# Four key tiles of a group's product with V at one step of the slot instead of at four

## The reference

```python
q, k, v = layernorm(x) @ Wq.T, context @ Wk.T, context @ Wv.T   # 16 heads of 16 channels
scores = q . k * SCALE, causal mask (keys 0..511 only matter)
probs = softmax(scores); y = probs . v; x = x + tanh(g_xattn) * (y @ Wo.T + bo)
# experts: softmax of layernorm(x) @ gate_w.T, each of 8 experts takes the 128 best tokens of a batch,
# silu(x_in @ w_gate) * (x_in @ w_up) @ w_down, scaled and added back, times tanh(g_ffn)
```

## Time and profile before

| | us |
|---|---|
| median of 3 runs (lowest, highest) | 2138.99 (2138.17, 2143.24) |
| the profiled execution | 2140.27 |
| its span, first to last instruction | 2138.5 |
| PE busy in the span | 1984.6 |
| DVE busy | 1221.2 |
| ACT busy | 956.8 |

### The profile page before, as it was taken

One profiled execution on the slowest core, in us unless ns is written; L12 is line 12 of the kernel. 1 busy time (PEld: TensorE's weight loads), 2 busy tenths in 40 slices (PEclk: granted clock), 3 DMA queues, 4 the chain that ended last, 5 costly groups with the idle time before them and its releaser, 6 DMA issues.

```text
span 2138.5 us, 43770 instructions
## 1 busy us (share of the span) xinstructions
PE 1984.6 (93%) x15339; PEld 1222.1 (57%) x15464; DVE 1221.2 (57%) x2441; ACT 956.8 (45%) x1792; POOL 582.7 (27%) x490
## 2 busy tenths in 40 slices
PE   3899999999999999996599999999999999999997
PEld 2455555555555555553256566565656666665665
DVE  4767787787777777775643434334343434435332
ACT  2456555555556555654243433333333433334332
POOL 2112222222222222213323231323323232322312
PEclk9999999999999999997699999999999999999999
DMA  4543444434444443334222221322222231312212
GB/s 114 116 120 107 131 130 129 116 119 122 131 138 134 127 138 114 112 94 134 63 70 47 53 57 43 64 59 57 48 53 48 72 60 40 60 26 35 40 15 26
DMA packets 141569, 179.70 MB, mean 84 GB/s; under 512 B 23544, under 2 KB 123008, under 8 KB 141440
## 3 DMA queue, kind: packets, MB, share of 16 engines
q1 hardware_dynamic: 116864, 144.39, 22.7%
q0 software_dynamic: 24576, 33.57, 9.7%
HBM read 118.63 MB, written 58.72 MB: 83 GB/s over the span
## 4 chain that ended last, share of the span: by engine, by line
PE 48%; DVE 2%; DMA 1%; issue 1%; POOL 0%; ACT 0%; DVEq 0%; ACTq 0%; POOLq 0%
PE bank L986 10%; PE bank L987 10%; PE bank L985 10%; PE bank L1002 5%; PE bank L1000 5%; PE bank L1001 5%; PE bank L955 2%; PE bank L969 1%; DMA out<-y,row_now 1%; DVE top_at L1061 1%; DVE work L1064 1%; DVE top L1059 1%; DVE h L1108 0%; ACT h L1038 0%; POOL out L919 0%
## 5 line engine op out<-in xcount | busy, mean ns | idle before, releaser
L529 ACT ACTIVATE prob<-bank 128x512 f32<-128x512 f32 x640 | 378.2, 596 | 234.3 <-PE bank L418 223.3
L613 DVE TENSOR_REDUCE mx<-bank 128x1 f32<-128x384 f32 (+3 forms) x704 | 429.7, 635 | 87.9 <-PE bank L402 78.8
L919 POOL DMA_INDIRECT out<-y,row_now x128 | 201.6, 1575 | 705.3 <-ACT y L1046 681.0
L1108 DVE TENSOR_TENSOR h<-bank,silu 128x512 f32<-128x512 f32 x256 | 176.7, 690 | 345.2 <-PE bank L987 283.8
L1038 ACT ACTIVATE h<-h 128x512 bf16<-128x512 f32 x256 | 161.1, 629 | 392.5 <-DVE h L1108 392.5
L400 PE MATMUL bank<-ks,qs 96*128 96x128 bf16 (+3 forms) x1024 | 279.7, 306 | 48.5 <-DVE mx L613 31.0
L1111 DVE TENSOR_TENSOR h<-h 128x512 bf16<-128x512 f32 x256 | 177.3, 693 | 179.3 <-ACT h L1038 179.3
L1000 PE MATMUL bank<-downT,h 128*128 128x256 bf16 x1024 | 279.3, 273 | 0.0
L1002 PE MATMUL bank<-downT,h 128*128 128x256 bf16 x1024 | 279.3, 273 | 0.0
L1001 PE MATMUL bank<-downT,h 128*128 128x256 bf16 x1024 | 279.3, 273 | 0.0
L416 PE MATMUL bank<-qs,ks 98*128 98x512 bf16 (+3 forms) x1024 | 267.2, 300 | 0.1
(11 more groups left out here) (152 smaller groups left out, 2912.5 us busy)
## 6 DMA issues: line engine op xcount, KB each, us to landing
qs<-q_parts SPq DMA_DIRECT2D x384, 64.0 KB, 2.6
ks<-k_parts SPq DMA_DIRECT2D x384, 64.0 KB, 2.7
q_parts<-q_sb SPq DMA_DIRECT2D x32, 384.0 KB, 3.1
k_parts<-k_sb SPq DMA_DIRECT2D x32, 384.0 KB, 3.2
x_t<-in_x SPq DMA_DIRECT2D x16, 512.0 KB, 4.0
ctx_t<-in_ctx SPq DMA_DIRECT2D x16, 512.0 KB, 4.9
res_t<-in_x SPq DMA_DIRECT2D x16, 512.0 KB, 5.5
out<-x SPq DMA_DIRECT2D x16, 512.0 KB, 3.1
```

Source lines behind the costliest of these rows:

```text
L529: nc.scalar.activation(prob[:, gr % 2, h0:h0 + nh, POFF[tiles[0]]:POFF[tiles[0]] + w], sc_bank[SC_BANK[k]][:, 0:nh * w].rearrange("p (h w) ...
L613: nc.vector.tensor_reduce(mx[:, gr % 2, h0:h0 + nh, i], max_bank[(gr * NMAX + k) % 2][:, 0:nh * w].rearrange("p (h w) -> p h w", h=nh), AX ...
L919: nc.gpsimd.indirect_dma_start(out_rows, bass.IndirectOffsetOnAxis(ap=row_now[:, par, CHUNK * c + s:CHUNK * c + s + 1], axis=0), y[:, c % ...
```

## The change

The four tiles of a group are issued one behind the other at one step: group 0 in slot 3 at step 4, group 1 in slot 0 at step 1, group 2 in slot 1 at step 3, group 3 in slot 2 at step 3. `pv+` of the groups moves to slot 3 step 6, slot 0 step 3, slot 1 step 5 and slot 2 step 5. What each tile computes and what it waits for stay.

```diff
+def group_pv(b, gr):
+
+    return [("pv", b, gr, j) for j in range(NT)]
...
-        0: {0: [("pv", b - 1, 1, 0), ("ln1+", b + 1, 0)], 1: [("yt", b - 1, 0), ("pv", b - 1, 1, 1)],
+        0: {0: [("ln1+", b + 1, 0)], 1: [("yt", b - 1, 0)] + group_pv(b - 1, 1),
             2: [("yt+", b - 1, 0), ("yb", b - 2, 1)],
-            3: [("pv", b - 1, 1, 2), ("mrow", b - 1, 3), ("yb+", b - 2, 1)],
+            3: [("pv+", b - 1, 1), ("mrow", b - 1, 3), ("yb+", b - 2, 1)],
             4: [("mt+", b - 1, 3), ("mt", b - 1, 3)],
-            5: [("pv", b - 1, 1, 3), ("o+", b - 2, 0), ("o", b - 2, 0, 0), ("o", b - 2, 0, 1), ("ln1+", b + 1, 1)],
-            6: [("pv+", b - 1, 1)],
+            5: [("o+", b - 2, 0), ("o", b - 2, 0, 0), ("o", b - 2, 0, 1), ("ln1+", b + 1, 1)],
...
-            3: [("pv", b - 1, 2, 0), ("mt+", b, 0), ("ln2", b - 2, 0)],
+            3: group_pv(b - 1, 2) + [("mt+", b, 0), ("ln2", b - 2, 0)],
             4: [("q", b + 1, 0, 0), ("q", b + 1, 0, 1), ("q+", b + 1, 0)],
-            5: [("pv", b - 1, 2, 1), ("ln2", b - 2, 1)],
+            5: [("pv+", b - 1, 2), ("ln2", b - 2, 1)],
             6: [("q", b + 1, 1, 0), ("q", b + 1, 1, 1), ("q+", b + 1, 1)],
-            7: [("pv", b - 1, 2, 2), ("tc", b + 1, 0), ("tc+", b + 1, 0)], 8: [("mrow", b, 0), ("tc", b + 1, 1)],
-            9: [("pv", b - 1, 2, 3), ("xs", b - 2), ("ln2+", b - 2, 1)],
-            10: [("pv+", b - 1, 2), ("ln2+", b - 2, 0), ("pv", b - 1, 3, 0), ("tc+", b + 1, 1)]},
-        2: {1: [("stack", b, 3), ("qstore", b + 1), ("mt", b, 1), ("mt+", b, 1), ("pv", b - 1, 3, 1)],
+            7: [("tc", b + 1, 0), ("tc+", b + 1, 0)], 8: [("mrow", b, 0), ("tc", b + 1, 1)],
+            9: [("xs", b - 2), ("ln2+", b - 2, 1)],
+            10: [("ln2+", b - 2, 0), ("tc+", b + 1, 1)]},
+        2: {1: [("stack", b, 3), ("qstore", b + 1), ("mt", b, 1), ("mt+", b, 1)],
             2: [("yt+", b - 1, 2), ("mrow", b, 1)],
-            3: [("yt", b - 1, 2), ("yb", b - 1, 0), ("yb+", b - 1, 0), ("k+", b + 1, 0)],
-            4: [("k", b + 1, 0, 0), ("k", b + 1, 0, 1), ("pv", b - 1, 3, 2)],
-            5: [("k", b + 1, 1, 0), ("pv", b - 1, 3, 3), ("load", b + 2), ("k+", b + 1, 1), ("k", b + 1, 1, 1)],
-            7: [("pv+", b - 1, 3), ("vaug", b)], 8: [("xt+", b - 2, 0), ("res", b - 1), ("xt", b - 2, 0)],
+            3: [("yt", b - 1, 2), ("yb", b - 1, 0), ("yb+", b - 1, 0), ("k+", b + 1, 0)] + group_pv(b - 1, 3),
+            4: [("k", b + 1, 0, 0), ("k", b + 1, 0, 1)],
+            5: [("k", b + 1, 1, 0), ("pv+", b - 1, 3), ("load", b + 2), ("k+", b + 1, 1), ("k", b + 1, 1, 1)],
+            7: [("vaug", b)], 8: [("xt+", b - 2, 0), ("res", b - 1), ("xt", b - 2, 0)],
...
-            4: [("pv", b, 0, 0), ("ll", b - 2), ("v", b + 1, 0, 0), ("v", b + 1, 0, 1), ("v+", b + 1, 0)],
-            5: [("ln1", b + 2, 0)], 6: [("stack", b + 1, 0), ("lt", b - 2), ("lt+", b - 2), ("pv", b, 0, 1)],
-            8: [("v+", b + 1, 1), ("v", b + 1, 1, 0), ("pv", b, 0, 2), ("v", b + 1, 1, 1)],
-            9: [("stack", b + 1, 1)], 10: [("pv+", b, 0), ("pv", b, 0, 3), ("save", b - 2), ("ln1", b + 2, 1)]},
+            4: group_pv(b, 0) + [("ll", b - 2), ("v", b + 1, 0, 0), ("v", b + 1, 0, 1), ("v+", b + 1, 0)],
+            5: [("ln1", b + 2, 0)], 6: [("stack", b + 1, 0), ("lt", b - 2), ("lt+", b - 2), ("pv+", b, 0)],
+            8: [("v+", b + 1, 1), ("v", b + 1, 1, 0), ("v", b + 1, 1, 1)],
+            9: [("stack", b + 1, 1)], 10: [("save", b - 2), ("ln1", b + 2, 1)]},
```

## The result

The changed kernel takes 2172.26 us (median of 4 runs, 2167.54 to 2175.29) against 2138.58 before (median of four): ratio 1.0146, 95% interval 1.0128 to 1.0164. The forecast was 2170 in 2150 to 2196. The profiled execution took 2167.54, span 2165.7.

The account below looks back on a forecast made before the run. PE bounds some attention stretches and DVE others, coupled by two max banks. Stretches 13.3 + 16.7 + 18.4 + 12.0 = 60.4 us against 57.8, +34 over thirteen batches, edges -3: 2171, median 1.3 lower, 2170 us (2150 to 2196).

Parts of the forecast that it names:

- The switch: PV blocks: some 0.24 us each independent of columns; merging turns 3.06 us a group into 2.39, 0.67 saved.
- Rival (b): PV blocks: switch not saved, or a 0.11 us weight load waited for at three boundaries; 2187 to 2205 us; chance 0.13.
- The four stretches: Attention-loop period cut after yb (slot 0), before PV (1), after yb (2), before v (3); sum 60.4 against 57.8 us.
- The third: Slot 2's yb to slot 3's v: 15.46 us grows to 18.4, two merged blocks standing where DVE has nothing to do.
- its other four terms: Slot 2 yb to slot 3 v: PV 2.39, to k product's end 1.86, DVE 3.18, last piece to v 7.88 us.
- One sign: PE's waits for maxima at least doubled, above all from step 8 of slot 1 to step 2 of slot 2.
- DVE has 19% idle overall: Rival that PE sets everything, DVE keeping up with 19% idle: faster, 2088 us, chance 0.12; partly, 2139, chance 0.08.
- Slot 0: yb to PV of slot 1: o starts at 3.11 us, new wait some 1.4 us, stretch 12.99 to 13.3.
- The edges: 12 groups in the edge bodies, lighter DVE: may save up to 0.67 us each, 8 us; taken as -3.
- +31: Whole kernel: +34 us for thirteen batches at +2.6, -3 for the edge bodies; on the profiled run's 2140.27 gives 2171.
- Rival (c): Attention loop: granted clock drops to 0.50 behind dense waits once per batch, 13 x 1.6 = +20 us, 2190; chance 0.17.
- The last stretch: Slot 3, v to yb: PV blocks of 3.96 us become 2.39, DVE holds PE 0.7; 12.84 falls to 12.0.

Follow-up runs that it names:

- e2: Changed kernel with group 2 alone back at its four steps of slot 1, pv+ at step 10: 2161.78 us, ratio 1.0104 to the kernel before.
- e3: Changed kernel with group 3 alone back at slot 1 step 10 and slot 2 steps 1, 4, 5: 2153.4 us, ratio 1.0069 to the kernel before.
- e6: Changed kernel with group 1 alone back at slot 0 steps 0, 1, 3, 5, pv+ at 6: 2159.96 us, ratio 1.0098.
- e4: Changed kernel, merged blocks re-placed: group 2 slot 1 step 6, group 3 slot 2 step 0, group 0 slot 3 step 6, group 1's pv+ behind ynT: 2134.31 us.
- e8: e7 with group 3's block behind the k products (slot 2 step 7) and group 1 apart: 2127.63 us, ratio 0.9945 to the kernel before.
- e1: Changed kernel with ACT copying group 1's PV bank (pv+) behind the high part of ynT instead of ahead: 2163.78 us, ratio 1.011.
- e9: e7 with group 1 apart (slot 0 steps 0, 1, 3, 5) as in the kernel before: 2117.66 us, ratio 0.9887 to the kernel before.
- e10: e9 with SP issuing the next batch's twelve group 0 stack loads ahead of the maxima row (slot 3 step 2, not 6): 2111.42 us, ratio 0.987.
- e11: Kernel before with only the copy to v_aug moved on DVE from slot 2 step 7 to slot 3 step 3: 2143.39 us, ratio 1.0009.
- e7: e4 with the copy to v_aug moved on DVE from slot 2 step 7 to slot 3 step 3: 2122.01 us, ratio 0.9919 to the kernel before.

## Why the prediction was right

*The switch.* 2.38 us per merged group was forecast as 2.39. Within the block nothing is waited for: from the start of its first tile (534.44) to the start of its last (536.40) 1152 columns take 1.96 us, 1.70 ns each, and 1280 at the forecast's 1.667 ns are 2.13; the remaining 0.25 is the switch in and out. Rival (b) is refuted.

So is, for this case, the rule of the Trainium skill ("TensorE: Matmul & The Clock Gate", Part 3) that a load overlaps matmuls in flight only where the row group differs: the heads differ here in columns alone, and their new weights cost no gap.

*The four stretches.* Forecast 13.3, 16.7, 18.4, 12.0; measured 13.33, 16.65, 18.19, 12.06. The third was 0.2 too high: the second rest of k on DVE came 2.87 us behind the first k product (558.12 - 555.25) and not 3.11; its other four terms were met within 0.02. e2, e3 and e6 show the mechanism behind the sum one group at a time, and e4 and e8 that it is the place and not the merging: a tile costs little where PE waits for maxima (three tiles of 1.98 us cost 0.4 in e2) and nearly its full length where DVE has run out of them (e3). One sign came out by halves: the waits for maxima were to double at least, and by the weight loads' rows they rose by a factor of 1.8, by the matmuls' rows by 2.5. And "DVE has 19% idle overall" was misread: by the earlier trace rows it is busy for 45.35 of 57.79 us, 22% idle; nothing hangs on it.

*Slot 0.* o was forecast 3.11 us behind yb's end and started at 3.21 (524.23 - 521.02). e1 confirms the order on ACT as the larger part of the new wait.

*The edges.* Forecast -3 us, measured about 0: batches 2 to 14 grew by 30.3 us together (2.3 each, forecast 34), and the attention phase as a whole (first step 0 to last PV) by 30.4. The two errors cancel. What follows the last PV was not changed and yet took 1158.6 us against 1162.2, with 3.5 us less of it at a granted clock of 0.50; so the profiled executions differ by 27.3 us, where +31 was forecast. The median lies 4.7 us above the profiled execution, so the agreement to 2 us is better than the working deserves.

*The clock.* Rival (c) didn't come about in the profiled execution: the granted clock was 1.00 through the loop. The others have no trace. The four executions took 2167.54 and 2169.41 us at a mean granted clock of 0.980, 2175.11 at 0.978 and 2175.29 at 0.976, so some of the 4.7 us may be the clock's; where it fell in those two is not known. The mechanism and its price are real. In e6, one batch shows them (windows as above):

```profile
541.47:544.60 3.13, 1.91 (x20) 1.26 (x21) 3.13 (x8) 1.46 (x4) 1.04 (x1) 1.00 0.45 138
544.60:548.01 3.41, 3.41 (x18) 2.66 (x19) 1.52 (x4) 1.19 (x2) 2.12 (x1) 0.50 0.50 148
```

Behind 3.1 us in which PE was busy for 1.9, the clock was 0.50 (1.2 GHz) for 3.41 us, and slot 2 of that batch took 18.42 instead of 16.80: 1.6 us, the price that was forecast, but in one batch of the loop and not in each.

*What the working lacked.* It had slot 3 bound by PE and DVE alone: in its words PV blocks of 3.96 us give way to 2.39 and DVE holds PE for 0.7. The landings told under e9, and e10, show SP's queue as what ends slot 3 in both kernels: DVE's part of the maxima row starts 3.13 us into the slot in both, 10.1 us later step 0 begins, and the slot is 13.1 to 13.5 us in both. The last stretch is shorter because v starts later in a slot of the same length; that 12.0 fitted is partly luck.

## What to carry to other kernels

Work on the fullest engine can be nearly free: where that engine waits for another's results, small pieces between the waits cost little, and gathering them to save a fixed cost (0.68 us a group) lost 34 us in this kernel until the gathered blocks stood where the other engine had a queue of its own. Cut one period at points that the change leaves alone, add up per stretch what each engine must do between two waits, and ask of every moved piece what it covered where it was and what it uncovers where it goes. When a wait moves instead of going, look at the queue that issues (here SP's twelve loads), not only at the data's chain.

## What was not expected of the hardware

The copy to v_aug (128x1024, f32 to f32, DVE) takes 1.58 us in the kernel before and 0.68 in e11. In the kernel before POOL is at work beside it:

```profile
544.81 1.58 DVE L678 COPY v_aug<-v_new 128x1024 f32<-128x1024 f32 x1
...
544.00 0.61 POOL L735 CAST k_sb<-rest 128x512 bf16<-128x512 f32 x1 [1.08 <-DVE rest L633]
544.69 1.15 POOL L737 TENSOR_TENSOR k_sb<-rest,k_sb 128x512 bf16<-128x512 f32 x1
```

DVE's copy begins at 544.81 and ends 0.55 us behind POOL's subtraction, which ends at 545.84; in e11 no POOL instruction runs beside any of the sixteen copies and all take 0.67 to 0.68. In e10 a single copy meets one and takes 1.38. The Trainium skill ("SBUF — State Buffer", "SBUF: two separate sides") says that DVE in a two-port mode and GpSimd hold a shared pair of ports one at a time, and the one that comes second is blocked for the other's whole instruction. The times agree with it, at 0.9 us a copy (in e10's single case too the copy ends 0.56 us behind POOL's subtraction); no row shows in which mode the copy ran. The 0.9 is about what e7 gained in slot 2; how much of that gain is the port and how much the place was not separated.
